# Other tiles for the gathered rows' split and for half of the expert weights, in a kernel of attention and routed experts

## The reference

```python
def _L0_attn_ref(x, ln_w, ln_b, Wq, bq, Wk, bk, Wv, bv, Wo, bo):   # x (8, 1024, 256), 16 heads of 16
    xn = (x - mu) * jax.lax.rsqrt(var + LN_EPS) * ln_w + ln_b
    q, k, v = proj(Wq, bq), proj(Wk, bk), proj(Wv, bv)
    q, k = _apply_rope(q, cos, sin), _apply_rope(k, cos, sin)
    attn = jax.nn.softmax(jnp.einsum('bhqd,bhkd->bhqk', q, k) / jnp.sqrt(jnp.float32(hd)), axis=-1)
    return x + jnp.einsum('bhqk,bhkd->bhqd', attn, v).transpose(0, 2, 1, 3).reshape(B, N, D) @ Wo.T + bo

def _L0_ffn_ref(x, gate_w, Wg, Wu, Wd):                            # 8 experts, inner width 512
    affinity = jax.nn.softmax(jnp.einsum('bsd,de->bse', x, gate_w), axis=-1)
    gating, index = jax.lax.top_k(jnp.transpose(affinity, (0, 2, 1)), K)      # K = 256 rows
    x_sel = x[b_idx, index]
    h = jax.nn.silu(jnp.einsum('bekd,edi->beki', x_sel, Wg)) * jnp.einsum('bekd,edi->beki', x_sel, Wu)
    out = jnp.einsum('beki,eid->bekd', h, Wd)
    return jnp.zeros_like(x).at[b_idx, index].add(out * gating[..., None])

xn = _layernorm(x, axis=-1)
x = x + _L0_attn_ref(xn, ...) + _L0_ffn_ref(xn, ...)
```

## The kernel before

| tile | start | bytes | in the expert part before |
|---|---|---|---|
| `w_hi0` to `w_hi3`, `w_lo0` to `w_lo3` | 21152 to 35488 | 2048 each | h's low part (`h_lo`) in four of them, output projection's weights |
| `zn_hi` | 71104 | 8192 | even experts: high part of gate, then of up |
| `zn_lo` | 79296 | 8192 | even experts: high part of down, then low part of gate |
| `parts0` | 108320 | 8192 | even experts: low part of up, then of down |
| `parts1` | 116512 | 8192 | rows: `x_hi`, then `x_lo` |
| `q_stack0`, `q_stack1` | 132896, 141088 | 8192 each | odd experts: gate high, up high; down high, gate low |
| `k_stack0` | 149280 | 8192 | odd experts: up low, down low |
| `k_stack1` | 157472 | 8192 | h's high part (`h_hi`) |
| `at_hi0` | 212896 | 2048 | stationary operand of the output projection |

## Time and profile before

### The profile page before, as it was taken

The page is one execution under the profiler, slowest core; times in us unless marked ns, Lnnn a source line. Parts: engine busy times, 40 slices in busy tenths (PEclk is TensorE's granted clock), DMA queues, the critical chain, the costliest instruction groups (busy, mean ns, idle before and its releaser), DMA issues.

```text
span 1777.1 us, 28942 instructions
## 1 busy us (share of the span) xinstructions
PE 1697.7 (96%) x11240; PEld 970.3 (55%) x11240; DVE 1034.8 (58%) x2056; ACT 1198.3 (67%) x1416; POOL 509.2 (29%) x480
## 2 busy tenths in 40 slices
PE   4499999999999999999999999899999999999997
PEld 4133344433434434434434433248888888888886
DVE  8646457456557558557647649747555454555543
ACT  3399988898898898898898889873333333333322
POOL 2101201111111111112111100025565656565653
PEclk9699999999999999999999999899999999999998
DMA  3634566558457457465475465535453434444332
GB/s 115 189 57 92 143 123 132 128 129 153 112 123 156 118 131 142 117 151 119 112 151 108 106 155 93 100 94 137 96 102 54 101 55 101 89 67 90 64 55 30
DMA packets 113458, 195.03 MB, mean 110 GB/s; under 512 B 20880, under 2 KB 59152, under 8 KB 113296
## 3 DMA queue, kind: packets, MB, share of 16 engines
q1 hardware_dynamic: 84112, 142.48, 36.2%
q0 software_dynamic: 29184, 50.35, 14.7%
HBM read 116.22 MB, written 76.55 MB: 108 GB/s over the span
## 4 chain that ended last, share of the span: by engine, by line
PE 87%; DVE 7%; DMA 2%; ACT 1%; issue 1%; POOL 1%; SPq 0%; DVEq 0%; ACTq 0%; POOLq 0%
PE o_ps L967 24%; PE score L1041 20%; PE score L953 18%; PE side L840 5%; PE score L1053 5%; PE o_ps L1053 3%; PE side L850 3%; PE side L1053 2%; PE side L881 2%; PE side L824 2%; PE score L1028 1%; DVE stats L1089 1%; DMA k_stack<-k_parts 1%; ACT probs L757 1%; DVE rot L1190 1%
## 5 line engine op out<-in xcount | busy, mean ns | idle before, releaser
L757 ACT ACTIVATE probs<-score 128x1024 f32<-128x1024 f32 x1024 | 974.9, 1037 | 144.5 <-PE score L953 142.7
L967 PE MATMUL o_ps<-probs,v_ones 128*32 128x512 f32 x4096 | 508.5, 605 | 7.8 <-DVE o_sb L1385 7.5
L953 PE MATMUL score<-q_stack,k_stack 50*128 50x512 f32 x2048 | 408.1, 463 | 17.3 <-DMA k_stack<-k_parts 11.1
L953 PEld LDWEIGHTS score<-q_stack,k_stack 50*128 50x128 f32 x2048 | 165.4, 186 | 362.2 <-ACT probs L757 299.5
L741 ACT ACTIVATE probs<-score 128x512 f32<-128x512 f32 x128 | 76.6, 598 | 335.0 <-PE score L1041 335.0
L668 POOL DMA_INDIRECT out<-probs,rot x128 | 204.3, 1596 | 212.2 <-DVE probs L1348 182.9
L967 PEld LDWEIGHTS o_ps<-probs,v_ones 128*32 128x32 f32 x4096 | 101.7, 109 | 229.0 <-issue 146.7
L1333 DVE TENSOR_TENSOR probs<-score,probs 128x512 f32<-128x512 f32 x128 | 88.5, 691 | 208.4 <-PE score L1041 180.9
L646 POOL TENSOR_TENSOR square<-qk 128x512 bf16<-128x512 f32 x56 | 77.2, 1407 | 398.8 <-DVE qk L1196 398.8
L1041 PE MATMUL score<-parts,q_stack 128*128 128x512 f32 x640 | 158.2, 389 | 0.0
L657 POOL DMA_INDIRECT qk<-xn_rows,rot x128 | 134.3, 1049 | 38.3 <-issue 29.3
(11 more groups left out here) (247 smaller groups left out, 2556.4 us busy)
## 6 DMA issues: line engine op xcount, KB each, us to landing
q_parts<-parts SPq DMA_DIRECT2D x16, 1024.0 KB, 4.3
k_parts<-parts SPq DMA_DIRECT2D x16, 1024.0 KB, 7.3
q_stack<-q_parts SPq DMA_DIRECT2D x62, 256.0 KB, 7.3
k_stack<-k_parts SPq DMA_DIRECT2D x62, 256.0 KB, 9.5
q_stack<-q_parts SPq DMA_DIRECT2D x66, 128.0 KB, 8.1
k_stack<-k_parts SPq DMA_DIRECT2D x66, 128.0 KB, 8.8
o_sums<-o_sb SPq DMA_DIRECT2D x256, 32.0 KB
num<-o_sums SPq DMA_DIRECT2D x32, 256.0 KB
```

The lines of the kernel that those rows point to most:

```text
L757: act.activation(probs[probs_of(s)][:, 2 * i:2 * i + 2, :], score[ring_of(p)][:, :, :], ACT.Exp, scale=SCALE).then_inc(exp_done, 1)
L953: last = pe.matmul(score[ring_of(p)][:, w, :], k_stack[par][rows, i, kt * P:(kt + 1) * P], q_stack[par][rows, i, qh * HALF:(qh + 1) * HALF ...
L967: last = pe.matmul(o_ps[j * KEYS_W:(j + 1) * KEYS_W, :], v_ones[par][:, kt, j, :], probs[probs_of(s)][:, j, :], start=kt == 0, stop=kt == ...
```

## The change

`x_hi` and `x_lo` lie in the two halves of `zn_hi` instead of those of `parts1`. Even experts' gate and up high parts lie in the two halves of `parts1` instead of those of `zn_hi`. All other tiles stay where they are, odd experts' weights included, and so do all starts in the table above. Each of the three high parts of expert 0 gets a wait on ACT, until all transfers out of `parts0` and `parts1` are done.

```diff
-    we_hi = [[wide(zn_hi[:, 0, :]), wide(zn_hi[:, 1, :]), tall(zn_lo[:, 0, :])],
+    high_part = parts[1][:, :, :, :].rearrange("p k a n -> p k (a n)")
+    we_hi = [[wide(high_part[:, 0, :]), wide(high_part[:, 1, :]), tall(zn_lo[:, 0, :])],
              [wide(q_stack[0][:, 0, :]), wide(q_stack[0][:, 1, :]), tall(q_stack[1][:, 0, :])]]
...
-    x_hi, x_lo = parts[1][:, 0, :, :], parts[1][:, 1, :, :]
+    x_hi, x_lo = (zn_hi[:, i, :].rearrange("p (c n) -> p c n", c=DC) for i in range(2))
...
                         act.wait_ge(side_free, last_jobs.base)
+                        act.wait_ge(parts_out, NB * 2 * PARTS_DMA)
                         high_weights(0, m)
```

## The result

The changed kernel takes 1778.58 us at the median of 7 runs, the kernel before 1773.36 us at the median of 7 beside it. The ratio is 1.0035 with a 95% interval of 1.0023 to 1.0047: 0.35% slower, 4 to 8 us, with 5.2 us between the medians. The direction and the size are those of rival B. The forecast, no change, was wrong, and the median lies 0.08 us above the stated range.

A forecast was written before the change was run, and what follows sets the result against it. PE was taken to bound the kernel, busy throughout the expert windows read. The terms summed to 0 to +1.5 us, taken as 0, so the median stayed at 1773.0 us, range 1767.5 to 1778.5.

The forecast's parts named there:

- rival B: Odd experts' `gate_up`: fast pace needs rows and weights aligned modulo a small power of two; +5.1 us, 1778.1 us, chance 0.23.
- What bounds the kernel: Expert part: PE alone sets the pace; even units take 17.92 us, odd 17.60, with 0.28 us of the difference in `gate_up`.
- The waits, the casts, `down` and `turn`: Expert part: three added ACT waits taken as 0 (0.4 us at most); moved casts, `down` and `turn` cost nothing more.
- Even experts' `gate_up`: 768 matmuls with exchanged tiles: stay slow, operands all in the lower part; 0 to +1.5 us, taken as 0.
- Odd experts' `gate_up`: 768 matmuls with rows moved to `zn_hi`: stay at 227 ns, stacks still high; taken as 0, upper bound +4.6 to +6.1 us.
- A's order in memory: Even experts' `gate_up`: fast when weights lie behind rows, so 5.1 us less, 1767.9 us; chance 0.20.
- the place has no say: Even experts are slow for another reason than place; 1773 us within 1 us, chance 0.07 shared with both rivals at once.

The follow-up runs named there:

- the first experiment: Kernel before with five small tiles (352 bytes) declared ahead of `xnT`, aligning `zn_hi` and `zn_lo` modulo 256 bytes: 1769.43 against 1776.76 us, ratio 0.9960.

## Why the prediction was wrong

**What bounds the kernel** held. PE alone sets a unit's time, and the difference between even and odd units, 0.32 us with 0.28 in `gate_up`, was the thing to look at.

**The waits, the casts, `down` and `turn`** held. The gap after the cast stays 0.14 us, ACT and DVE keep their work, and in the changed kernel the rest of a unit stays near 6.7 us (17.93 - 11.20 in expert 2, 17.93 - 11.23 in expert 3).

**Even experts' `gate_up`** held at 0: 11.17 to 11.20 us. The bounds were 227 and 235 ns, and it stayed at 233, though for another reason than the one given.

**Odd experts' `gate_up`** is the term that failed. Its bounds, 0 and +4.6 to +6.1 us, did hold the +5.4 that came. The value taken, 0, rested on the step "Each slow pair has both of its operands in the lower part of the partition, under 124704 bytes; each fast pair has one there and one above 132896". That was a true description of the pairs in the trace and the wrong cause. With every tile in the same half as before, a move of 352 bytes makes the even pace fast, and a pad of 32 bytes makes the odd pace slow; and in the changed kernel odd experts are slow with rows low and weights high.

**The weighing of rival B** failed in one argument: that loads of up's low part from `parts0` agree with `parts1`, and yet their two matmuls take 0.47 us. The fact was right. What it was read for assumed that each load costs by itself. With `zn_lo` alone off, the slow steps spread to loads that agree, and in the kernel before ten of twelve loads were off, so the two that agree could not be expected to show a fast pace. That row was no evidence against B. Of the others, A's order in memory is excluded by the changed kernel itself, where all weights lie behind the rows and all units are slow, and that the place has no say is excluded by the first experiment.

**The size** was right once the mechanism is: B was priced at 1778.1 us with a rise to 17.92 us a unit; units rose to 17.94 and the median is 1778.58, from a median before of 1773.36 instead of 1773.0. The range ended 0.4 us above B's time, which left nothing for that.

The rule on the two ports, in the Trainium skill's "TensorE: Matmul & The Clock Gate", "Step-by-step: what each phase is for", by which a weight load takes no read bandwidth from the running matmul, was rightly set against the row. The runs put a number to it: with a load beside each matmul of 512 columns, a pair of operands whose starts do not agree modulo 256 bytes costs 6 to 7 ns on top of 227. No run leaves the loads out, so that it is the load's reading that disturbs the stream is argued and not shown.

## What to carry to other kernels

When the same instruction with the same shape has two paces, look at where its operands start, as differences modulo small powers of two, before looking at how far apart they are. A theory on placement can be tried for nothing, by moving small tiles in the order of declaration; keep in mind that everything behind a pad moves with it, and other stages may gain or lose. And an exception inside a mixed row (an aligned pair that is slow among others that are not aligned) is weak evidence, since a delay can pass on to its neighbours, as with `zn_lo` alone off: judge rows that are alike throughout.

## What the runs showed of the hardware

For back-to-back fp32r matmuls of 128 x 128 by 512 columns, each with a weight load of its own, at a granted clock of 1.00, the pace is 226.8 to 227.3 ns where moving and stationary operands start at the same place modulo 256 bytes of the partition, and 232 to 234 ns where they are 32, 64 or 128 bytes off; in the kernel before and in the changed one the slow pairs that decide are 96 bytes off, or 160 counted the other way. An aligned row settles at the fast pace after one step in some kernels and after about five in others, and one load in six that is off holds the row at 230.6. For 256 columns no gain from alignment was seen: the shortest `down`, 5.66 us, has `k_stack1` 32 and 128 bytes off from the down weights, against 5.80 and 5.83 us with these aligned. Why the period is 256 bytes, and what of the load and the stream meets there, no run shows; nor was it tried with bf16 or with fewer partitions.
